# Transposes of the unit matrix between two norms' tiles, a row tile mixed by VectorE alone, and half a unit of keys and values moved behind the branch products

## The chip, the cores and the metric

The kernel runs on one core of one Trainium2 chip. The metric is the device time of one execution in microseconds (us); three runs of the kernel before gave 1453.57, 1454.41 and 1455.25, a median of 1454.41.

## The reference, cut to what matters

Two decoder layers on x of 2 x 256 rows by 512, each of three blocks (self-attention, a block on a context of 2 x 512 rows, a feed-forward block), and each block is followed by `x = layernorm(x + block(x))`. Six such norms are counted here from 0. The change acts in and around these:

```python
# layer 0, third block ("mixing"), then norm 2
H_res, H_pre, H_post = logits of (x * rsqrt(mean(x*x))) @ [W_res, W_pre, W_post].T
H_res = sinkhorn_log(H_res)            # 50 iterations on 4x4 per row
H_res = (1 - g) * I + g * H_res
x_pre = einsum('btnc,btn->btc', x_streams, softmax(H_pre))
y = x_pre @ W_branch
x_mixed = einsum('btij,btjc->btic', H_res, x_streams)     # 4 streams of 128 columns
block = x_mixed + einsum('btc,btn->btnc', y, softmax(H_post))
x = layernorm(x + block)               # norm 2

# layer 1, first block: a gated linear attention; it begins with
dt = softplus(x @ Win.T + dt_bias);  g = dt * A           # 32 heads
x = layernorm(x + l1_attention(x))     # norm 3

# layer 1, second block: cross-attention to the context
q = x @ Wq.T;  k = ctx @ Wk.T;  v = ctx @ Wv.T            # 8 groups of keys and values
```

The keys and values of the cross-attention depend on the context alone, so the kernel computes them early, beside the Sinkhorn iterations.

## The kernel before

The 512 rows are four tiles of 128 rows (`t` = 0 to 3), held in `x`; `xT` holds the columns as rows. The programs of the engines are written out one by one, in the order in which each engine works, and semaphores tie them together; there is no scheduler. The order of each engine's program is thus the order of the calls at the end of the kernel (`block.tensor` for TensorE, and so on).

**Norm n** runs in two pairs of tiles (`PAIRS`). VectorE takes the statistics (`ln_spread`), GpSimd the power (`ln_gpsimd`, L718), VectorE scales the two tiles (`ln_rows`, L712), TensorE transposes each in four pieces (`ln_tensor`, L725), and ScalarE copies the result to `xT` (`ln_scalar`, L765). After norm 3 ScalarE writes a high part and VectorE the low part (L737), and the cross-attention's queries (L192 to L194, three products of parts for each) start when both are there.

**The mixing layer.** TensorE computes the logits from `xT` pair by pair (`mix_logits`, L945) and the branch products of all four tiles (`mix_branches`, L953, one bank of `BRANCH_BANKS` for each tile). VectorE runs 50 Sinkhorn iterations in five windows (`sink_rounds`, L1138, L1142, L1144), GpSimd gathers the factors (L1129), and between two windows ScalarE takes their logarithm (L1195) and a new exponential (L1197), for which VectorE waits. ScalarE scales the branch products (`branch_pre`, L1152), TensorE sums them (`mix_branch_sums`, L1824), and ScalarE writes the result of each stream to `tmp[4 + t]` (`branch_post`, L1159). At the end of the iterations VectorE mixes the four streams of each tile: ScalarE has made the products of streams 0 and 1 (`mix_streams`, L997), VectorE those of streams 2 and 3 with a running sum (L1108) and adds ScalarE's two (L1100). The statistics of norm 2 (L1088) stand between the tiles.

**Keys and values.** There are 32 units (8 groups of 4), each sixteen 128x256 products on TensorE that fill a bank (`kv_unit`, L1803) and two copies on ScalarE (`kv_copy`, L1838). Units 0 and 1 stand ahead of the loop, in banks 0 and 3 (`kv_tensor_first`, `KV_FIRST`), the rest in `kv_tensor` alternates between banks 2 and 7, so a unit waits for the copy of the one two before it. ScalarE's copies are dealt out over the five windows of the Sinkhorn iterations by `KV_WINDOWS`; a window's copies, the branch work and `mix_streams` all stand in its queue ahead of the window's logarithm:

```python
KV_WINDOWS = [3, 5, 5, 6, 11]
for i, count in enumerate(KV_WINDOWS):
    for k in range(count):
        kv_copy(act, unit)
        ...
        if i == 4 and k in (5, 6):
            mix_streams(act, 2 * (k - 5))
            mix_streams(act, 2 * (k - 5) + 1)
```

**After norm 2** TensorE computes the product for dt (`dt_tensor`, L1272, 32x512 in four steps of the contraction), then the values, keys and queries of the first attention group; VectorE and ScalarE make dt's running sums, which go through memory (`g_rows`) and come back as rows for the decays.

Of the kernel before, what the change touches and what calls it, by code (L numbers as in the profile page):

```python
# [14 lines left out]
P = 128  # L15
# [20 lines left out]
def decoder_kernel(nc, a, out):  # L36

    sems = {}
    with ExitStack() as ctx:
# [248 lines left out]

        FILLERS = 10

        def l0_tensor(pe):
# [645 lines left out]

        BRANCH_BANKS = [1, 3, 4, 5]

# [17 lines left out]
        def mix_scalar(act):  # L957
            for k in range(2):
                for t in PAIRS[k]:
                    act.wait_ge(sem("ln_x"), NT * 1 + t + 1)  # L960
                    act.activation(tmp[t][:, :], x[:, t, :], ACT.Square, accum_out=ssq[:, 0, t:t + 1])\
                       .then_inc(sem("mix_ssq"), 1)
                ln_scalar(act, 1, k)
                if k == 0:
                    kv_copy(act, 1)

# [23 lines left out]
        def mix_streams(act, t):  # L990

            if t == 0:
                act.wait_ge(sem("mix_ready"), 3)
                act.wait_ge(sem("branch"), NT + 1)
# [6 lines left out]
        def mix_vector(dve):  # L1001
# [89 lines left out]
            for t in range(NT):  # L1091
                acc = tmp[4 + t]
                at = [0] * STREAMS
                for j in (2, 3):
                    xj = x[:, t, j * P:(j + 1) * P]
                    if j == STREAMS - 1:
                        dve.wait_ge(sem("vector_step"), tally[0])
                        dve.wait_ge(sem("branch_part"), 2 * NT + t + 1)
                        for part in mixed:
                            step(dve, dve.tensor_tensor(acc[:, :], acc[:, :], part[t], ALU.add))  # L1100
                        at = [tally[0]] * STREAMS
                    for i in range(STREAMS):
# [53 lines left out]
        def branch_post(act, t):  # L1156

            for i in range(STREAMS):
                last = act.activation(tmp[4 + t][:, i * P:(i + 1) * P], bank[6][:, t * P:(t + 1) * P],  # L1159
                                      ACT.Copy, scale=soft[:, 0, t * 8 + 4 + i:t * 8 + 5 + i])  # L1160
            last.then_inc(sem("branch_part"), 1)

        def sink_scalar(act):
# [10 lines left out]
            act.activation(h, h, ACT.Exp).then_inc(sem("sink_h"), 1)  # L1174
            unit = len(KV_FIRST)
            for i, count in enumerate(KV_WINDOWS):
                for k in range(count):
# [8 lines left out]
                    if i == 3 and k < 2:  # L1186
                        branch_post(act, k + 2)
                    if i == 4 and k in (5, 6):
                        mix_streams(act, 2 * (k - 5))
                        mix_streams(act, 2 * (k - 5) + 1)  # L1190
                if i < SINK_ITERS // SINK_BLOCK - 1:
# [561 lines left out]
        KV_BANKS = [2, 7]  # L1753
        KV_WINDOWS = [3, 5, 5, 6, 11]
        KV_FIRST = [0, 3]
# [63 lines left out]
        def mix_branch_sums(pe):  # L1819

            for t in range(NT):
                pe.wait_ge(sem("branch_part"), t + 1)
                for j in range(STREAMS):
                    last = pe.matmul(bank[6][:, t * P:(t + 1) * P], ident[:, :], tmp[t][:, j * P:(j + 1) * P],  # L1824
                                     start=(j == 0), stop=(j == STREAMS - 1))
# [757 lines left out]
        def _(pe):  # L2583
# [11 lines left out]
            ln_tensor(pe, 1, 0)  # L2595
            kv_tensor_first(pe, 1, (0, 1))
            mix_logits(pe, 0)
            ln_tensor(pe, 1, 1)
            mix_logits(pe, 1)
            mix_branches(pe)  # L2600
            kv_tensor(pe)
            ln_tensor(pe, 2, 0)
            pe.wait_ge(sem("kv_copied"), 4 * NG)
            ln_tensor(pe, 2, 1)
            dt_tensor(pe)
            l1_tensor(pe)
            for k in range(2):
                ln_tensor(pe, 3, k)
            pe.wait_ge(sem("low_part"), L1_LOW + KC + NG + NT)
# [107 lines left out]
```

## Time and profile before

| | us |
|---|---|
| three runs | 1453.57, 1454.41, 1455.25 |
| profiled execution | 1456.52 |
| its span, first to last instruction | 1454.0 |
| TensorE busy | 1404.8 (97%) |
| VectorE busy | 1065.0 (73%) |
| ScalarE busy | 872.7 (60%) |
| GpSimd busy | 590.3 (41%) |
| share of the chain that ended last | TensorE 70%, VectorE 14%, ScalarE 5%, GpSimd 4% |

The profile is one execution of the program. Times are us from the span's start. PE is TensorE's matmul side, PEld its weight loads, DVE VectorE, ACT ScalarE, POOL GpSimd, SP SyncE. "Granted clock" is the share of full speed that TensorE was allowed; 1.00 is 2.4 GHz and 0.50 is 1.2 GHz. Ends of matmuls are modelled, so starts are the better marks. Where a row has "[a <-b]", the engine was idle for a us before it, until b.

### The profile page before, as it was taken

The numbers are of one execution on the slowest core, as the hardware profiler recorded it, in microseconds if no ns is written. First come the engines' busy times: TensorE is split into PE (matmuls) and PEld (weight loads), VectorE is DVE, ScalarE is ACT, GpSimd is POOL, SyncE is SP. The second block draws the span as 40 slices with busy tenths as digits, with TensorE's granted clock in tenths as the row PEclk, the third lists the DMA queues.
The fourth block names the chain that finished last, engine by engine and source line by source line (L and its number), as shares of the span: only waits on it lengthen the run. The fifth ranks groups of instructions, "written<-read, shape, count | busy, mean of one in ns | idle before, by whom it ended". The sixth has DMA issues, their size and how long they took to land.

```text
span 1454.0 us, 24444 instructions
## 1 busy us (share of the span) xinstructions
PE 1404.8 (97%) x7666; PEld 1175.8 (81%) x7666; DVE 1065.0 (73%) x2471; ACT 872.7 (60%) x2194; POOL 590.3 (41%) x631
## 2 busy tenths in 40 slices
PE   8999999999999899999999999889999999999997
PEld 7888888887788767778788788678888888888875
DVE  5697667687787876766776776767788788777885
ACT  5556555655423456755755755647677677677661
POOL 3555444444122136555645645425243242242221
PEclk9999999999999989999999999989999999999999
DMA  8011110112123230321322221320111012012000
GB/s 325 1 73 73 73 71 2 71 34 102 59 89 128 99 135 30 130 102 42 119 101 76 82 102 59 131 77 25 36 67 74 16 73 87 15 72 79 1 1 30
DMA packets 30135, 107.75 MB, mean 74 GB/s; under 512 B 3847, under 2 KB 13191, under 8 KB 22104
## 3 DMA queue, kind: packets, MB, share of 16 engines
q1 hardware_dynamic: 30040, 106.58, 20.0%
q8 instruction: 47, 0.77, 0.2%
q14 instruction: 48, 0.39, 0.1%
HBM read 97.07 MB, written 9.50 MB: 73 GB/s over the span
## 4 chain that ended last, share of the span: by engine, by line
PE 70%; DVE 14%; issue 6%; ACT 5%; POOL 4%; DMA 0%; DVEq 0%; POOLq 0%; ACTq 0%; SPq 0%
PE bank L192 14%; PE bank L193 14%; PE bank L194 14%; PE bank L1803 5%; PE bank L1974 3%; POOL wq_low L1244 2%; PE bank L336 2%; PE bank L1989 2%; PE bank L1995 2%; PE bank L359 2%; PE bank L1991 2%; PE bank L305 2%; PE bank L1932 1%; DVE logit L2286 1%; PE bank L347 1%
## 5 line engine op out<-in xcount | busy, mean ns | idle before, releaser
L165 POOL TENSOR_TENSOR tmp<-tmp,sin 128x512 f32<-128x512 f32 x80 | 106.5, 1332 | 220.0 <-ACT tmp L150 218.1
L194 PE MATMUL bank<-wo_low,att_high 128*128 128x512 f32 x384 | 150.7, 392 | 0.0
L2286 DVE SCALAR_TENSOR_TENSOR logit<-bank,qss,amask 128x512 f32<-128x512 f32 x128 | 91.0, 747 | 58.7 <-PE bank L194 57.6
L2192 POOL TENSOR_TENSOR qss<-qss,half 128x4 f32<-128x4 f32 x32 | 34.9, 1091 | 201.2 <-DVE qss L2272 201.2
L1803 PE MATMUL bank<-kT,wg 128*128 128x256 f32 x512 | 113.7, 384 | 2.9 <-ACT prob L1838 2.9
L2093 ACT ACTIVATE prob<-logit,rmax 128x512 f32<-128x512 f32 x128 | 91.6, 719 | 38.7 <-DVE rmax L2290 38.7
L1803 PEld LDWEIGHTS bank<-kT,wg 128*128 128x128 f32 x512 | 97.9, 192 | 17.4 <-ACT prob L1838 3.7
L149 ACT ACTIVATE tmp<-bank 64x512 f32<-64x512 f32 x80 | 47.6, 595 | 103.8 <-PE bank L194 98.1
L192 PE MATMUL bank<-l_wo_high,att_high 128*128 128x512 f32 x256 | 104.6, 408 | 1.8 <-DVE att_low L1687 1.1
L193 PE MATMUL bank<-xT_high,wq_low 128*128 128x512 f32 x256 | 103.4, 404 | 0.0
L193 PE MATMUL bank<-l_wo_high,att_low 128*128 128x512 f32 x256 | 99.8, 390 | 0.0
L2107 ACT ACTIVATE p_high<-bank 128x512 fp32r<-128x512 f32 x128 | 70.1, 597 | 45.6 <-PE bank L1974 45.2
L580 DVE TENSOR_TENSOR logit<-bank,keys 128x384 f32<-128x384 f32 x64 | 35.5, 555 | 73.2 <-PE bank L338 73.2
L194 PEld LDWEIGHTS bank<-wo_low,att_high 128*128 128x128 f32 x384 | 72.1, 188 | 16.6
L2304 DVE TENSOR_TENSOR p_low<-bank,p_high 128x512 fp32r<-128x512 f32 x128 | 81.8, 681 | 0.1
L2290 DVE TENSOR_REDUCE rmax<-logit 128x2 f32<-128x1024 f32 x64 | 78.1, 1220 | 2.2
L448 ACT ACTIVATE prob<-logit,rmax 128x128 f32<-128x128 f32 (+1 forms) x128 | 57.4, 449 | 33.4 <-DVE rmax L584 33.3
L228 DVE TENSOR_TENSOR x<-x,bank 128x512 f32<-128x512 f32 x96 | 64.7, 680 | 17.2 <-PE bank L194 16.6
L2099 ACT ACTIVATE prob<-prob,rsum 128x512 f32<-128x512 f32 x64 | 46.4, 724 | 39.7 <-DVE rsum L2295 39.7
L1989 PE MATMUL bank<-p_high,v_high 128*128 128x256 f32 x256 | 67.9, 297 | 2.1 <-ACT p_high L2107 2.1
L1974 PEld LDWEIGHTS bank<-ident,prob 128*128 128x128 f32 x512 | 59.4, 140 | 11.9 <-issue 2.3
L1974 PE MATMUL bank<-ident,prob 128*128 128x128 f32 x512 | 67.5, 273 | 1.5 <-DVE k_low L2260 1.4
(321 smaller groups left out, 4393.5 us busy)
## 6 DMA issues: line engine op xcount, KB each, us to landing
wq<-in_l_wq SPq DMA_DIRECT2D x16, 1024.0 KB, 5.8
wo<-in_l_wo SPq DMA_DIRECT2D x16, 1024.0 KB, 4.9
wkv<-in_l_wkv SPq DMA_DIRECT2D x16, 512.0 KB, 5.7
wg<-in_l_wg SPq DMA_DIRECT2D x8, 1024.0 KB, 4.8
wq<-in_x_wq SPq DMA_DIRECT2D x8, 1024.0 KB, 7.1
wo<-in_x_wo SPq DMA_DIRECT2D x8, 1024.0 KB, 4.9
kT<-in_x_wkv SPq DMA_DIRECT2D x8, 512.0 KB, 3.9
kv_keys<-logit SPq DMA_DIRECT2D x8, 512.0 KB, 4.4
```

The costliest lines, as they stand in the source:

```text
L165: eng.tensor_tensor(halves(tmp[4 + j % 2]), halves(tmp[2 + j % 2]), per_batch(sin), ALU.mult).then_inc(sem(f"{l}_sinp"), 1)
L192: eng.matmul(dst, a_high, b_high, start=start, stop=False)
L193: eng.matmul(dst, a_low, b_high, start=False, stop=False)
L194: return eng.matmul(dst, a_high, b_low, start=False, stop=stop)
L1803: last = pe.matmul(dst[:, i * 256:(i + 1) * 256], wg[t // CT][:, c, t % CT * P:(t % CT + 1) * P], weights[:, c, :], start=(c == 0), stop=( ...
L1974: last = pe.transpose(bank[5 + half_][:, kt * L + c * P:kt * L + (c + 1) * P], prob[s % 2][:, c, (2 * half_ + kt) * P:(2 * half_ + kt + 1) ...
L1989: pe.matmul(dst, v_high[at][:, b * CT + kt, :], p_high[s % 2][:, kt, :], start=(kt == 0), stop=False)
L2093: last = act.activation(prob[s % 2][:, c, :], logit[s % 2][:, c, :], ACT.Exp, bias=rmax[s % 2][:, c:c + 1], accum_out=rsum[s % 2][:, c:c + 1])
L2107: act.activation(p_high[s % 2][:, 2 * half_:2 * half_ + 2, :].rearrange("p a b -> p (a b)"), bank[5 + half_][:, :], ACT.Copy).then_inc(sem ...
L2286: dve.scalar_tensor_tensor(logit[s % 2][:, c, :], bank[3 + c][:, :], qss[p][:, 1, h, 2 * b + c:2 * b + c + 1], amask[:, c, :], ALU.mult, A ...
L2290: dve.tensor_reduce(rmax[s % 2][:, 0:2], logit[s % 2][:, :, :], AX.X, ALU.max, negate=True)\
L2304: dve.tensor_tensor(p_low[s % 2][at].rearrange("p a b -> p (a b)"), bank[5 + half_][:, :], p_high[s % 2][at].rearrange("p a b -> p (a b)") ...
```

## The change

- A helper `keep_busy` issues transposes of the unit matrix into a bank that nobody reads. In norm 2, 14 of them stand behind the first pair of tiles and 6 behind the second. In norm 3, 16 stand behind the first pair, after a wait for the last residual sum of tile 2 (whose bank they write), and 11 behind the second pair.
- The second half of unit 1 moves behind the branch products; its copy moves from ScalarE's norm 1 into the first window. The branch banks change to 1, 4, 5 and 6, since bank 3 is still in use, and the branch sums go to bank 1.
- The windows of copies become 5, 5, 5, 6 and 10.
- VectorE makes all four streams of tile 0; ScalarE makes streams 0 and 1 of tiles 1, 2 and 3 only, one tile behind each of three copies, the first of them one copy earlier in the window.

```diff
+        def keep_busy(pe, n, dst):
+            for _ in range(n):
+                pe.transpose(dst[:, 0:P], ident[:, :], ident[:, :])
...
-        BRANCH_BANKS = [1, 3, 4, 5]
+        BRANCH_BANKS = [1, 4, 5, 6]
+        BRANCH_SUMS = 1
...
                 ln_scalar(act, 1, k)
-                if k == 0:
-                    kv_copy(act, 1)
...
         def mix_streams(act, t):
-            if t == 0:
+            if t == 1:
                 act.wait_ge(sem("mix_ready"), 3)
...
-                for j in (2, 3):
+                for j in (range(STREAMS) if t == 0 else (2, 3)):
                     xj = x[:, t, j * P:(j + 1) * P]
                     if j == STREAMS - 1:
                         dve.wait_ge(sem("vector_step"), tally[0])
-                        dve.wait_ge(sem("branch_part"), 2 * NT + t + 1)
-                        for part in mixed:
-                            step(dve, dve.tensor_tensor(acc[:, :], acc[:, :], part[t], ALU.add))
-                        at = [tally[0]] * STREAMS
+                        if t:
+                            dve.wait_ge(sem("branch_part"), 2 * NT + t)
+                            for part in mixed:
+                                step(dve, dve.tensor_tensor(acc[:, :], acc[:, :], part[t], ALU.add))
+                            at = [tally[0]] * STREAMS
...
-            unit = len(KV_FIRST)
+            unit = 1
...
-                    if i == 4 and k in (5, 6):
-                        mix_streams(act, 2 * (k - 5))
-                        mix_streams(act, 2 * (k - 5) + 1)
+                    if i == 4 and k in (4, 5, 6):
+                        mix_streams(act, k - 3)
...
-        KV_WINDOWS = [3, 5, 5, 6, 11]
+        KV_WINDOWS = [5, 5, 5, 6, 10]
...
             ln_tensor(pe, 1, 0)
-            kv_tensor_first(pe, 1, (0, 1))
+            kv_tensor_first(pe, 1, (0,))
             mix_logits(pe, 0)
             ln_tensor(pe, 1, 1)
             mix_logits(pe, 1)
             mix_branches(pe)
+            kv_tensor_first(pe, 1, (1,))
             kv_tensor(pe)
             ln_tensor(pe, 2, 0)
+            keep_busy(pe, 14, bank[1])
             pe.wait_ge(sem("kv_copied"), 4 * NG)
             ln_tensor(pe, 2, 1)
+            keep_busy(pe, 6, bank[1])
             dt_tensor(pe)
             l1_tensor(pe)
-            for k in range(2):
-                ln_tensor(pe, 3, k)
+            ln_tensor(pe, 3, 0)
+            pe.wait_ge(sem("l1_added"), 4 * (NG - 1) + 3)
+            keep_busy(pe, 16, bank[L1_OUT[2]])
+            ln_tensor(pe, 3, 1)
+            keep_busy(pe, 11, bank[L1_OUT[2]])
```

**TensorE from norm 1 to the units of keys and values**, before (L725 is a tile's transposes, L1803 products of a unit, L945 the logits, L953 a tile's branch products):

```order
L725 MATMUL bank6<-ident,x 128x128 x4
L725 MATMUL bank5<-ident,x 128x128 x4
L1803 MATMUL bank3<-kT0,wg0 128x256 x8
L945 MATMUL bank0<-wmix,xT 128x24 x8
L725 MATMUL bank7<-ident,x 128x128 x4
L725 MATMUL bank2<-ident,x 128x128 x4
L945 MATMUL bank0<-wmix,xT 128x24 x8
L953 MATMUL bank1<-branch,xT 128x128 x4
L953 MATMUL bank3<-branch,xT 128x128 x4
L953 MATMUL bank4<-branch,xT 128x128 x4
L953 MATMUL bank5<-branch,xT 128x128 x4
L1803 MATMUL bank2<-kT0,wg1 128x256 x8
```

The same place in the change, where the lines are L730, L1807, L951 and L959:

```order
L730 MATMUL bank6<-ident,x 128x128 x4
L730 MATMUL bank5<-ident,x 128x128 x4
L1807 MATMUL bank3<-kT0,wg0 128x256 x4
L951 MATMUL bank0<-wmix,xT 128x24 x8
L730 MATMUL bank7<-ident,x 128x128 x4
L730 MATMUL bank2<-ident,x 128x128 x4
L951 MATMUL bank0<-wmix,xT 128x24 x8
L959 MATMUL bank1<-branch,xT 128x128 x4
L959 MATMUL bank4<-branch,xT 128x128 x4
L959 MATMUL bank5<-branch,xT 128x128 x4
L959 MATMUL bank6<-branch,xT 128x128 x4
L1807 MATMUL bank3<-kT0,wg0 128x256 x4
```

Four of the eight products of unit 1 in bank 3 have moved from ahead of the first logits to behind the last branch products. (A row counts the products of the program; the profile has two records for such a product.)

**VectorE at the start of the mix**, before (L1108 multiplies and adds, L1100 adds ScalarE's products):

```order
L1108 SCALAR_TENSOR_TENSOR tmp4<-x,hres,tmp4 128x128 x4
L1100 TENSOR_TENSOR tmp4<-tmp4,tmp0 128x512
L1100 TENSOR_TENSOR tmp4<-tmp4,xT 128x512
L1108 SCALAR_TENSOR_TENSOR x<-x,hres,tmp4 128x128 x4
L1108 SCALAR_TENSOR_TENSOR tmp5<-x,hres,tmp5 128x128 x4
```

and in the change (L1113 and L1105):

```order
L1113 SCALAR_TENSOR_TENSOR tmp4<-x,hres,tmp4 128x128 x12
L1113 SCALAR_TENSOR_TENSOR x<-x,hres,tmp4 128x128 x4
L1113 SCALAR_TENSOR_TENSOR tmp5<-x,hres,tmp5 128x128 x4
L1105 TENSOR_TENSOR tmp5<-tmp5,tmp1 128x512
L1105 TENSOR_TENSOR tmp5<-tmp5,xT 128x512
```

Tile 0 has lost its two additions of ScalarE's products and gained eight products of its own; tile 1 is as before.

**TensorE at norm 2**, in the change (L730 are the tiles' transposes, L294 those of the unit matrix, L1276 the product for dt):

```order
L730 MATMUL bank6<-ident,x 128x128 x4
L730 MATMUL bank5<-ident,x 128x128 x4
L294 MATMUL bank1<-ident 128x128 x14
L730 MATMUL bank7<-ident,x 128x128 x4
L730 MATMUL bank2<-ident,x 128x128 x4
L294 MATMUL bank1<-ident 128x128 x6
L1276 MATMUL bank7<-xT,win 32x512 x4
```

The rows of L294 are new; before, the four rows of transposes and the product for dt followed each other directly.

## Rows read from the trace of the kernel before

**Rows 1.** The page, 40 slices of the span: granted clock in tenths.

```profile
PEclk9999999999999989999999999989999999999999
```

**Rows 2.** Timeline, all engines: start, us, engine, line, operation, shapes, idle before.

```profile
380.50 3.62 PE L1803 MATMUL bank<-kT,wg 128*128 128x256 f32 x16
...
383.31 1.00 DVE L712 TENSOR_SCALAR x<-x,mv,lnr 128x512 f32<-128x512 f32 x2 [0.81 <-POOL lnr L718]
383.96 1.86 PE L945 MATMUL bank<-wmix,xT 128*128 128x24 f32 x16
...
384.70 0.63 ACT L961 ACTIVATE tmp<-x 128x512 f32<-128x512 f32 x1
...
386.33 1.08 ACT L765 ACTIVATE xT<-bank 128x512 f32<-128x512 f32 x2 [0.30 <-PE bank L725]
```

**Rows 3.** Timeline: TensorE's unit 7, and ScalarE's second and fourth logarithm.

```profile
411.94 5.41 PE L1803 MATMUL bank<-kT,wg 128*128 128x256 f32 x16 [2.07 <-ACT prob L1838]
...
429.11 0.23 ACT L1195 ACTIVATE zsm<-fac 128x32 f32<-128x32 f32 x1 [0.58 <-POOL fac L1129]
...
466.79 0.23 ACT L1195 ACTIVATE zsm<-fac 128x32 f32<-128x32 f32 x1 [0.28 <-POOL fac L1129]
```

**Rows 4.** Timeline: the mix, 486 to 505 us.

```profile
486.33 1.14 DVE L1108 SCALAR_TENSOR_TENSOR tmp<-x,hres,tmp 128x128 f32<-128x128 f32 x4
...
487.12 1.27 ACT L997 ACTIVATE tmp<-x,hres 128x128 f32<-128x128 f32 x4
...
489.65 0.69 DVE L1100 TENSOR_TENSOR tmp<-tmp 128x512 f32<-128x512 f32 x1 [2.19 <-ACT xT L997]
...
492.24 1.13 DVE L1108 SCALAR_TENSOR_TENSOR tmp<-x,hres,tmp 128x128 f32<-128x128 f32 x4
...
497.69 7.17 PE L1803 MATMUL bank<-kT,wg 128*128 128x256 f32 x32 [0.80 <-ACT prob L1838]
```

**Rows 5.** Timeline: norm 2 and the product for dt.

```profile
506.25 1.11 PE L725 MATMUL bank<-ident,x 128*128 128x128 f32 x8 [1.39 <-DVE x L712]
...
506.95 1.08 ACT L765 ACTIVATE xT<-bank 128x512 f32<-128x512 f32 x2 [1.39 <-PE bank L725]
...
509.18 1.94 PE L725 MATMUL bank<-ident,x 128*128 128x128 f32 x8 [1.82 <-DVE x L712]
...
511.90 5.50 PE L1272 MATMUL bank<-xT,win 128*32 128x512 f32 x8 [0.78 <-ACT xT L765]
```

**Rows 6.** Windows: length, busy PE, PEld, DVE, ACT, POOL; granted clock, DMA, GB/s.

```profile
506.20:508.90 2.70, 1.11 (x8) 0.84 (x8) 1.85 (x6) 1.08 (x2) 0.70 (x1) 1.00 0.97 361
509.00:515.60 6.60, 5.64 (x13) 2.45 (x14) 3.13 (x7) 5.04 (x11) 0.00 (x0) 0.50 0.46 171
...
956.20:962.80 6.60, 5.62 (x13) 4.46 (x14) 2.12 (x4) 0.19 (x2) 0.00 (x0) 0.50 0.20 86
...
932.20:935.50 3.30, 2.91 (x14) 2.94 (x14) 1.45 (x6) 0.00 (x0) 2.90 (x3) 0.50 0.96 333
935.70:937.00 1.30, 1.30 (x15) 1.30 (x13) 0.75 (x1) 1.30 (x8) 0.38 (x1) 1.00 0.95 372
1416.90:1420.30 3.40, 2.35 (x16) 1.81 (x15) 1.51 (x4) 2.93 (x7) 2.41 (x2) 1.00 0.00 0
```

**Rows 7.** Timeline: transposes of TensorE in two of these stretches.

```profile
934.43 1.06 PE L1451 MATMUL bank<-ident,q 128*128 128x128 f32 x4
...
1417.35 1.09 PE L1974 MATMUL bank<-ident,prob 128*128 128x128 f32 x8
```

**Rows 8.** Timeline: norm 3's second pair and the first query product.

```profile
954.51 1.11 PE L725 MATMUL bank<-ident,x 128*128 128x128 f32 x8 [2.58 <-DVE x L712]
...
957.18 0.80 PE L192 MATMUL bank<-xT_high,wq_high 128*128 128x512 f32 x1 [1.56 <-DVE xT_low L737]
```

**Rows 9.** The chain that ended last, the queries: start, us, line.

```profile
958.40 0.43 PE bank L194
...
963.06 0.23 PE bank L193
```

More of the change, by code:

```diff
@@ L1158, in branch_post @@
             for i in range(STREAMS):
-                last = act.activation(tmp[4 + t][:, i * P:(i + 1) * P], bank[6][:, t * P:(t + 1) * P],
+                last = act.activation(tmp[4 + t][:, i * P:(i + 1) * P], bank[BRANCH_SUMS][:, t * P:(t + 1) * P],
                                       ACT.Copy, scale=soft[:, 0, t * 8 + 4 + i:t * 8 + 5 + i])
@@ L1823, in mix_branch_sums @@
                 for j in range(STREAMS):
-                    last = pe.matmul(bank[6][:, t * P:(t + 1) * P], ident[:, :], tmp[t][:, j * P:(j + 1) * P],
+                    last = pe.matmul(bank[BRANCH_SUMS][:, t * P:(t + 1) * P], ident[:, :], tmp[t][:, j * P:(j + 1) * P],
                                      start=(j == 0), stop=(j == STREAMS - 1))
```

## The prediction

> **What bounds the kernel now.** I read the page first: the granted clock of TensorE is below 9 tenths in two slices of 40 only, the fifteenth and the twenty-seventh [rows 1], so on the whole TensorE is fed and runs at its upper level, 2.4 GHz. Those two slices hold norms 2 and 3. I then read the timeline where the change acts: the front of the mixing layer (380 to 389 us), the units of keys and values beside the Sinkhorn rounds (to 505 us), and the two norms. Up to 486 us two chains run side by side. VectorE does 50 Sinkhorn rounds and stops four times for a logarithm of ScalarE; TensorE does units of keys and values, each copied out by ScalarE. What ends last is VectorE: TensorE waits for its rows before the transposes of norm 2 [rows 5]. From there on TensorE, ScalarE and VectorE hand the work to each other, and the clock has fallen to 1.2 GHz: the stretch from 509.0 to 515.6 us is granted 0.50, behind one with 1.11 us of work in 2.70. So it is after norm 3, from 956.2 to 962.8 us [rows 6].
>
> **Part 1, half a unit of keys and values behind the branch products.** Before, unit 1 takes TensorE from 380.50 to 383.96, 3.46 us, and the transposes of tiles 2 and 3 stand behind it; ScalarE also copies it before it squares tile 2 at 384.70 [rows 2]. Now half of it (1.73) stands there: TensorE is free at 382.2, the first logits end at 383.9, and the transposes follow. VectorE's norm has tile 2 ready at 383.85 (383.31 and half of the 1.00 for two), so ScalarE squares from there. For both squares it needs some 1.3 us (384.70 to 386.33 less 0.30 idle), which puts the first column copy at 385.15 instead of 386.33. The logits end 1.2 us earlier, and so the Sinkhorn chain starts.
> How much of that reaches the end of the rounds depends on ScalarE's queue: a window's last copy stands ahead of the logarithm that VectorE waits for. TensorE starts the branch products 1.2 us earlier and does half a unit more behind them. With five copies in the first window instead of three it no longer waits 2.07 us before unit 7, nor does it run that unit in 5.41 us instead of 3.46 [rows 3], as that slow stretch follows the wait. So unit n+1 is done within 0.1 us of where unit n was. The windows also end one unit later (10, 15 and 21 instead of 9, 14 and 20): their last copies end at the old times, 428.5 and 466.5 (the logarithms of 429.11 and 466.79 less idle times of 0.58 and 0.28 [rows 3]). Of 1.2 us only 0.6 is then left at the second logarithm and 0.3 at the fourth. **The rounds end 0.3 us earlier** (bounds 0 and 0.6).
>
> **Part 2, tile 0 by VectorE alone.** Before, VectorE does one stream of tile 0 at 486.33 and then waits 2.19 us for ScalarE's products; two sums and the last stream bring it to tile 1 at 492.24, 5.91 us later [rows 4]. ScalarE copies a unit first and starts its products at 487.12. Now VectorE does sixteen products, 1.14 per four: 4.3 to 4.6 us. It saves 5.91 - 4.3 = 1.6 us. In that time ScalarE does tile 1 (eight products, two rows of 1.27), and it copies one unit between any two tiles, where pairs of tiles had made TensorE wait 0.80 us at 497.69 [rows 4]. Tiles 1 to 3 find their products ready. **The rows of norm 2 come 1.6 + 0.3 = 1.9 us earlier**: its transposes start at 504.35 instead of 506.25, and could at 507.3 instead of 509.18 [rows 5].
>
> **Part 3, norm 2.** TensorE's last unit now ends near 500.4 (504.86 less one unit of 3.46, less the wait of 0.80, plus bits), so it waits 4 us for VectorE instead of 1.39. I expect it to be at 1.2 GHz when the rows come, or to fall at once: 1.39 and 1.82 us of waiting [rows 5] were enough before. Eight transposes take 1.11 us at 2.4 GHz and 1.94 at 1.2 [rows 5], so 0.14 and 0.24 each. Behind the first eight stand 14 more. At full clock they take 1.9 us and just fit between the pairs of tiles; at half clock they take 3.4. In time: transposes to 506.3, ten fillers at 0.24 to 508.7, where I let the clock rise (an estimate: 0.50 lasted 3.3 us where work filled it, 6.6 where waits were in it [rows 6]), and four at 0.14: 509.25. That is where the second pair starts now: **the fillers eat the lead of 1.9 us**. But the second pair then runs at full clock: 1.78 us from its start to the end of ScalarE's second copy (506.25 to 506.95 + 1.08 for the first pair) and 0.13 to the next product, so 511.15 against 511.90. The six fillers (0.8) fit under those copies. The product for dt took 5.50 us from 511.90, of it 3.7 at 0.50 [rows 5, 6]; at full clock that is 3.5. It ends at 514.65 instead of 517.4. **Norm 2 gives 2.8 us.** Bounds: 4.7 if the clock never falls, 2.0 if it stays low through all the fillers and rises behind them. What follows (dt on VectorE, rows through memory, decays) starts from that product, and its other inputs move with it.
> Can such transposes hold or raise the clock? From 932.2 to 935.5 TensorE is granted 0.50 and ends that stretch with 1.06 us of transposes; behind it the clock is 1.00. From 1416.9 to 1420.3 it has 2.35 us of work, 1.09 of it transposes, and stays at 1.00 [rows 6, 7]. I take it that they count. The Trainium skill says otherwise: by "TensorE: Matmul & The Clock Gate", Part 4 (PE-mode transpose), the full clock does not come from transposes, which don't count as busy in the way of matmuls. By that rule this part would lose; rival 2 has the price, from rows.
>
> **Part 4, norm 3.** TensorE waits 2.58 us between the pairs of tiles and 1.56 before the queries [rows 8]. Sixteen fillers (2.2) fit into the first wait, eleven (1.5) into the second. The new wait, for the sum of tile 2, costs nothing: that sum feeds this norm and is done before tile 3's. The clock should hold. The queries start at 957.18 and step by 0.43 us, from 963.06 by 0.23 [rows 8, 9]: some thirteen steps that take 5.9 us and would take 3.3 with the slower first one. **It gives 2.5 us**; bounds 1.3 (the low stretch can fall shorter than here) and 2.9.
>
> **Sum.** 2.8 + 2.5 = 5.3 us off the profiled execution of 1456.5 (a span of 1454.0 and 2.5 around it): 1451.2. The median of the runs, 1454.4, lies 2.1 below that execution. The low stretches fall a little differently from run to run, so I take 5.0 off the median: **1449.4 us**. This case's own range is 1447.4 to 1451.4.
>
> **Rivals.**
> 1. *The fillers hold the clock but do not raise it* (12%). Norm 3 gives its 2.5. In norm 2 the clock is down after the wait of 4 us; fillers run to 509.7, the second pair to 511.6, six fillers to 513.1, the product takes 5 to 6 us: 518.1 to 519.1, a loss of 1.2. Together 1.3 faster: 1453.1. For it: no row shows transposes alone raising the clock. Against it: the row at 932.2.
> 2. *The fillers count for nothing and stand in the way at half speed* (10%), the slower side. Norm 2 loses up to 1.7 (519.1). In norm 3 the clock falls near 956 as before; eleven fillers take 2.6 instead of 1.5 and push the queries back by 1.1. Together 2.8 slower: 1457.2, and up to 1459 if the sixteen are caught too. It decides where 14 fillers at 0.24 outlast the gap of 1.8 us between the pairs.
> 3. *The clock stays up in norm 2 in spite of the wait* (8%): 4.7 + 2.5, so 1447.2.
> 4. *The gains are there, but behind norm 2 the gate weights or the rows through memory bind* (6%): norm 3's 2.5 alone, 1451.9.
>
> **How the numbers follow.** The forecast has 64%. A measurement of this kernel can tell about 0.2%, 2.9 us, from no change. Faster by more, below 1451.5: nearly all of the forecast, rival 3, a third of rival 4 and a tenth of rival 1: 0.73. Within it: most of rivals 1 and 4, half of 2: 0.21. Slower: half of rival 2 and one more in a hundred: 0.06. The range, 1447.0 to 1453.5, takes in the forecast and rivals 1, 3 and 4, and leaves out rival 2 and the tails.
>
> **What would show it.** In the changed profile: the Sinkhorn rounds start 1.2 us earlier, but the fourth logarithm only 0.3, right behind a copy; no stop of TensorE near 410 us; VectorE without a wait in the mix; TensorE idle for about 4 us before norm 2 and granted 0.50 there, its 14 fillers partly at 0.24; the dt product in 3.5 us; 1.00 throughout norm 3 and query steps of 0.23. Wrong would be: 0.50 to the end of the dt product (rivals 1, 2), query steps of 0.43 (rival 2), a wait of VectorE for ScalarE's products, or the logarithms later than before.

## The result, and the profile after

The changed kernel takes 1461.58 us (median of 20 runs), the kernel before 1454.53 (20 runs): a ratio of 1.0042 with a 95% interval of 1.0034 to 1.0049. It is slower; 1449.4 was forecast, with 1453.5 as the upper end. The profiled execution has a span of 1459.3 us against 1454.0. Where the 5.3 us arise, read from the timelines of the two executions (us from the start of each span):

| point in the program | before | after | difference |
|---|---|---|---|
| VectorE reads the logits (the rounds start) | 389.05 | 389.28 | +0.23 |
| last instruction of the rounds | 486.01 | 488.68 | +2.67 |
| first transposes of norm 2 | 506.25 | 507.37 | +1.12 |
| first product behind the dt product | 517.34 | 516.88 | -0.46 |
| first product of the last attention group | 879.11 | 885.89 | +6.78 |
| last group's second set of transposes (before L1451) | 937.22 | 945.47 | +8.25 |
| first query product | 957.18 | 965.45 | +8.27 |
| end of the span | 1454.0 | 1459.3 | +5.3 |

Step by step, the change gives 1.55 us in the mix, 1.58 in norm 2 and 2.97 from the first query product on (2.60 of it in the queries right behind norm 3, the rest because later low stretches of the clock fell elsewhere). It loses 0.23 ahead of the rounds, 2.44 in them, 7.24 among the attention groups, which it does not touch, and 1.47 in the last of these.

**The logits of norm 1.** Timeline of the changed kernel, TensorE and VectorE, and one window (length; busy PE, PEld, DVE, ACT, POOL; granted clock):

```profile
383.17 1.00 DVE L717 TENSOR_SCALAR x<-x,mv,lnr 128x512 f32<-128x512 f32 x2 [0.81 <-POOL lnr L723]
385.62 3.56 PE L951 MATMUL bank<-wmix,xT 128*128 128x24 f32 x16 [0.74 <-ACT xT L770]
389.00 5.50 PE L959 MATMUL bank<-branch,xT 128*128 128x128 f32 x32
389.28 0.69 DVE L1018 SCALAR_TENSOR_TENSOR mix<-bank,ssq,base 128x24 f32<-128x24 f32 x4 [3.99 <-PE bank L951]
...
385.80:392.40 6.60, 6.60 (x32) 6.60 (x33) 2.31 (x13) 1.04 (x5) 0.57 (x1) 0.50 0.00 0
```

The second logits product starts 1.36 us earlier than before (386.98, [rows 2]), but behind a wait of 0.74 us instead of 0.25, and the clock is 0.50 from 385.7 us for 6.8 us. The product takes 3.56 us instead of 1.97 and the branch products 5.50 instead of 3.82 (before: "388.79 3.82" in the same view), so the lead is gone, and units of keys and values start 1.89 us later (394.33 against 392.44).

**The logarithms.** ScalarE, second and fourth window:

```profile
431.20 0.38 ACT L1842 ACTIVATE prob<-bank 128x256 f32<-128x256 f32 x1
431.46 0.23 ACT L1199 ACTIVATE zsm<-fac 128x32 f32<-128x32 f32 x1
...
469.45 0.23 ACT L1199 ACTIVATE zsm<-fac 128x32 f32<-128x32 f32 x1
```

Both stand in ScalarE's queue with no idle time ahead of them (the row above the first is a unit's copy): it is the copies that VectorE waits for. They come 2.35 and 2.66 us later than those of [rows 3].

**The mix and norm 2.** VectorE, then TensorE, then two windows:

```profile
489.00 3.24 DVE L1113 SCALAR_TENSOR_TENSOR tmp<-x,hres,tmp 128x128 f32<-128x128 f32 x12
492.27 1.14 DVE L1113 SCALAR_TENSOR_TENSOR x<-x,hres,tmp 128x128 f32<-128x128 f32 x4
493.33 1.14 DVE L1113 SCALAR_TENSOR_TENSOR tmp<-x,hres,tmp 128x128 f32<-128x128 f32 x4
...
507.37 1.11 PE L730 MATMUL bank<-ident,x 128*128 128x128 f32 x8 [3.97 <-DVE x L717]
508.31 2.92 PE L294 MATMUL bank<-ident 128*128 128x128 f32 x14
511.03 1.51 PE L730 MATMUL bank<-ident,x 128*128 128x128 f32 x8
512.38 0.82 PE L294 MATMUL bank<-ident 128*128 128x128 f32 x6
513.36 3.59 PE L1276 MATMUL bank<-xT,win 128*32 128x512 f32 x8 [0.16 <-ACT xT L770]
...
508.70:511.90 3.20, 3.20 (x17) 3.20 (x17) 1.09 (x3) 0.44 (x1) 0.69 (x1) 0.50 0.61 241
512.20:517.00 4.80, 4.64 (x19) 1.68 (x17) 2.65 (x6) 4.80 (x11) 0.00 (x0) 1.00 0.00 0
```

VectorE no longer waits in the mix: tile 0 takes 4.33 us (489.00 to 493.33) instead of 5.91 [rows 4]. TensorE waits 3.97 us instead of 1.39 [rows 5], starts the transposes at full clock, falls to 0.50 at 508.6, and is at 1.00 again from 512.0. The dt product takes 3.59 us instead of 5.50.

**The loop over the attention groups.** Between two groups of layer 1, VectorE's timeline after, and its DMA queues from 736 to 753 us:

```profile
740.34 0.69 DVE L228 TENSOR_TENSOR x<-x,bank 128x512 f32<-128x512 f32 x1 [2.03 <-PE bank L194]
744.87 0.87 DVE L1699 COPY gc<-cols 128x40 f32 x1 [3.84 <-issue]
750.74 1.14 DVE L1646 SCALAR_TENSOR_TENSOR probT<-logit,gc,lower 128x128 f32<-128x128 f32 x4 [5.00 <-issue]
...
q14 instruction: 4, 0.03, 0.5%
```

and before, the same place (in its DMA view of that stretch there is no row of q14):

```profile
740.86 0.69 DVE L228 TENSOR_TENSOR x<-x,bank 128x512 f32<-128x512 f32 x1 [2.03 <-PE bank L194]
741.47 0.18 DVE L1695 COPY gc<-cols 128x40 f32 x1
741.89 1.14 DVE L1642 SCALAR_TENSOR_TENSOR probT<-logit,gc,lower 128x128 f32<-128x128 f32 x4 [0.24 <-DVE gc L1695]
```

"issue" is an idle time in which the engine waited for nothing that the profile shows. VectorE runs the middle four groups as a loop of two passes over two groups each (`piped_groups`, L138), 266 instructions a pass, and its only jump back lies here, in a stop of 3.84 us; one of 5.00 follows. Meanwhile four packets of 8 KB arrive on q14, a queue of instructions (the profile does not say of which engine), one of them within each stop. TensorE runs dry behind it and comes back at half clock:

```profile
756.22 0.79 PE L192 MATMUL bank<-l_wg_high,xT_high 128*128 128x512 f32 x1 [4.76 <-ACT tmp L152]
...
754.40:761.00 6.60, 4.78 (x11) 3.80 (x12) 5.88 (x10) 5.01 (x9) 3.46 (x3) 0.50 0.22 93
```

The group in which this happens takes 60.10 us, where all others but the first (44.8) take 52.8 to 52.9. Over the whole span the page counts 53 packets on q14 after and 48 before.

**Norm 3.** TensorE, after:

```profile
959.16 1.03 PE L730 MATMUL bank<-ident,x 128*128 128x128 f32 x8
960.03 1.91 PE L294 MATMUL bank<-ident 128*128 128x128 f32 x16
962.78 1.11 PE L730 MATMUL bank<-ident,x 128*128 128x128 f32 x8 [0.84 <-DVE x L717]
963.73 1.36 PE L294 MATMUL bank<-ident 128*128 128x128 f32 x11
965.45 0.50 PE L192 MATMUL bank<-xT_high,wq_high 128*128 128x512 f32 x1 [0.36 <-DVE xT_low L742]
965.79 0.40 PE L193 MATMUL bank<-xT_high,wq_low 128*128 128x512 f32 x1
...
955.00:972.00 17.00, 15.80 (x95) 13.36 (x94) 10.49 (x24) 4.57 (x13) 3.51 (x5) 1.00 0.34 125
```

The waits of 2.58 and 1.56 [rows 8] have become 0.84 and 0.36 and the clock is 1.00 throughout. The queries step by 0.23 from the second on, where thirteen of them stepped by 0.43 before [rows 9].

### The profile page after: what moved, and what is told of

Read it like the earlier page. It is cut to its first block, busy times and chain, and to the rows that moved or that the text cites. A ratio compares the mean times of both kernels' runs of the same rounds, so it can differ in the third digit from the quotient of the medians.

```text
span 1459.3 us, 24535 instructions
## 1 busy us (share of the span) xinstructions
PE 1409.5 (97%) x7713; PEld 1183.2 (81%) x7713; DVE 1065.7 (73%) x2477; ACT 870.3 (60%) x2186; POOL 590.0 (40%) x631
## 4 chain that ended last, share of the span: by engine, by line
PE 68%; DVE 15%; issue 6%; ACT 6%; POOL 4%; DMA 0%; DVEq 0%; ACTq 0%; POOLq 0%; SPq 0%
PE bank L192 13%; PE bank L193 13%; PE bank L194 13%; PE bank L1807 5%; PE bank L1978 3%; POOL wq_low L1248 2%; PE bank L341 2%; PE bank L1993 2%; PE bank L1999 2%; PE bank L364 2%; PE bank L1995 2%; PE bank L310 2%; DVE logit L2290 1%; PE bank L1936 1%; PE bank L352 1%
## 5 line engine op out<-in xcount | busy, mean ns | idle before, releaser
L1807 PE MATMUL bank<-kT,wg 128*128 128x256 f32 x512 | 111.4, 379 | 0.0
L1807 PEld LDWEIGHTS bank<-kT,wg 128*128 128x128 f32 x512 | 97.0, 190 | 13.3 <-issue 0.2
## 6 DMA issues: line engine op xcount, KB each, us to landing
wkv<-in_l_wkv SPq DMA_DIRECT2D x16, 512.0 KB, 5.9
kT<-in_x_wkv SPq DMA_DIRECT2D x8, 512.0 KB, 4.2
kv_keys<-logit SPq DMA_DIRECT2D x8, 512.0 KB, 4.7
```

Source lines behind the costliest of these rows:

```text
L1807: last = pe.matmul(dst[:, i * 256:(i + 1) * 256], wg[t // CT][:, c, t % CT * P:(t % CT + 1) * P], weights[:, c, :], start=(c == 0), stop=( ...
```

## The experiments

**Theory A: the place of VectorE's loop.** The change puts a few more instructions on VectorE ahead of the loop. Its body would then start at another place against the blocks in which instructions are fetched, and at a bad one the jump back would find part of the body gone. The rival: the stops come from the products, transposes or DMAs of the change. Both are separated by memsets of a column of a spare tile, which stand ahead of `dt_vector` and compute nothing.

*e1: the change with twelve such memsets; e2: the kernel before with five (the same lines with `range(5)`).*

```python
+            for i in range(12):
+                dve.memset(spare[:, i:i + 1], 0.0)
             dve.wait_ge(sem("ld_l1"), 16 * 4)
             dt_vector(dve)
```

> The changed kernel with twelve one-column memsets on VectorE between norm 2 and the product for dt, where VectorE waits. Theory A (VectorE's loop over the attention groups now lies so in its code that the jump back finds its first instructions gone and loads them again: two stops of 4 to 5 us at 740 and 746 us, with extra instruction packets at 737 to 752): the loop moves by 12 instructions, the stops go, group 4 takes 52.8 us instead of 60.1, and the kernel is 7 us faster than the change, about 1454 us, ratio to before 0.997 to 1.000. Rival B (the stops come from a late input or from DMA traffic at that time, not from where the code lies): they stay, ratio 1.004.

> The kernel before with five such memsets, about the number of instructions that the change adds ahead of VectorE's loop. Theory A: the same two stops appear in group 4 though nothing else of the change is there, 7 us slower, ratio about 1.005. Rival B: no stops, ratio 1.000.

e1: 1451.81 us (12 runs), 0.9988 of before (0.9976 to 0.9999), all groups behind the first 52.8 to 52.9. e2: 1460.49 us (5 runs), 1.0042 (1.0029 to 1.0055), with both stops. VectorE's timeline at the jump, e1 and then e2:

```profile
739.13 0.69 DVE L229 TENSOR_TENSOR x<-x,bank 128x512 f32<-128x512 f32 x1 [2.03 <-PE bank L195]
739.78 0.18 DVE L1700 COPY gc<-cols 128x40 f32 x1
740.21 1.14 DVE L1647 SCALAR_TENSOR_TENSOR probT<-logit,gc,lower 128x128 f32<-128x128 f32 x4 [0.24 <-DVE gc L1700]
```

```profile
737.63 0.69 DVE L229 TENSOR_TENSOR x<-x,bank 128x512 f32<-128x512 f32 x1 [2.03 <-PE bank L195]
742.10 0.93 DVE L1696 COPY gc<-cols 128x40 f32 x1 [3.78 <-issue]
747.80 1.14 DVE L1643 SCALAR_TENSOR_TENSOR probT<-logit,gc,lower 128x128 f32<-128x128 f32 x4 [4.77 <-issue]
```

Adding instructions takes the loss away, and five that do nothing bring it into the kernel before. The rival falls. (By medians e1 is 9.8 us faster than the change, and the group explains 7.3 of it. In e1's profile the clock also stayed up until the logits of norm 1 were through; the rest is not assigned.)

*e8 and e9: the kernel before with nine and with fourteen memsets.*

> The kernel before with nine memsets. If VectorE's code is loaded in blocks and what counts is how many blocks its loop body of 266 instructions touches, the bad positions are a run of about nine beginning at one to five more than before, so nine more is bad too: group 4 takes 60.1 us, span about 1460. If the position of five was a single bad one, it takes 52.8, span about 1454.

> Fourteen one-column memsets on VectorE ahead of its loop over groups, in the kernel before. If the place of the loop's body against blocks of fetched instructions decides (4.8 to 5 and 9 added instructions had the stops, 0 and, in another version, some 17 had not), 14 should lie past the bad stretch: all groups 52.8 us, no stop of VectorE of 3.8 and 4.8 us behind the branch, about 1454 us. If more instructions alone are bad, or if the count matters in another way, one group takes 60.1 us and the run 1460.

One run each: e8 1459.8 us, one group of 60.22, and the two stops are one of 9.85 us with two packets of q14 in it; e9 1454.67, all groups behind the first 52.8 to 52.9, no stop. So 0 is good, 5 and 9 are bad, 14 is good: what counts is the place, not that there are more instructions. What is shown is this, and that packets of an instruction queue arrive within the stops. That VectorE waits for them is the plain reading, but no run shows it directly. The Trainium skill, "Runtime: NRT & Kernel Launch", section "Instruction fetch mechanics", says that a taken branch to code outside a window of two pages must wait for a fetch; the stops agree with it. It gives blocks of 16 KiB with 256 instructions; the packets here carried 8 KB, which by its ratio is 128 instructions. Two estimates follow. In pages of 256, a body of 266 instructions lies in two pages or, from nine starts in 256, in three; in blocks of 128 it lies in three or, from nine starts in 128, in four. The four points fit a bad stretch of nine and do not tell the two apart; how many blocks VectorE holds was not measured.

**The parts, apart from it.** e3 and e4 leave the loop at its place of before; e5, e6, e7, e10, e11 and e12 have the twelve memsets. None of these eight shows the stops.

*e3: the fillers of norms 2 and 3 alone, in the kernel before.*

```python
             ln_tensor(pe, 2, 0)
+            keep_busy(pe, 14, bank[1])
...
             ln_tensor(pe, 2, 1)
+            keep_busy(pe, 6, bank[1])
...
+            keep_busy(pe, 16, bank[L1_OUT[2]])
...
+            keep_busy(pe, 11, bank[L1_OUT[2]])
```

> The kernel before with only the transposes of the unit matrix, 14 and 6 in norm 2, 16 and 11 in norm 3. Theory A (they hold the clock where the wait ahead of them is 1.4 us and not 4): granted clock 1.00 through both norms, second pair of norm 2 at 509.2, dt product in 3.5 us, queries in steps of 0.23: 2.8 + 2.5 us faster, ratio 0.9963. Rival C (transposes do not count as work for the clock): 0.50 as before in both, 0 to 3 us slower.

1451.07 us (10 runs), 0.9977 (0.9967 to 0.9986). TensorE in norm 2, and the window from there to the next group:

```profile
506.22 1.11 PE L730 MATMUL bank<-ident,x 128*128 128x128 f32 x8 [1.40 <-DVE x L717]
507.17 1.69 PE L294 MATMUL bank<-ident 128*128 128x128 f32 x14
509.15 1.06 PE L730 MATMUL bank<-ident,x 128*128 128x128 f32 x8 [0.29 <-DVE x L717]
510.05 0.82 PE L294 MATMUL bank<-ident 128*128 128x128 f32 x6
511.04 3.59 PE L1277 MATMUL bank<-xT,win 128*32 128x512 f32 x8 [0.17 <-ACT xT L770]
...
508.00:515.00 7.00, 6.54 (x33) 3.36 (x32) 3.97 (x8) 5.19 (x11) 0.42 (x1) 1.00 0.58 203
```

With the rows at the time of before (506.22), the clock is at 1.00, and the next product comes at 514.57 instead of 517.34: 2.77 us. Both norms were seen to gain as expected, but the ratio over the runs is 3.3 us (1454.95 x 0.0023), less than expected. The profiled span is 7.4 us shorter than before's: it is the second fastest of the ten runs, and it also lacks the low stretches of the clock that before has near 932 and 987 us.

This one execution does not show by itself that the fillers held the clock. In e2, which has none, the profiled execution has 1.00 throughout norm 2 as well (TensorE, and one window):

```profile
505.70 1.11 PE L726 MATMUL bank<-ident,x 128*128 128x128 f32 x8 [1.41 <-DVE x L713]
508.62 1.06 PE L726 MATMUL bank<-ident,x 128*128 128x128 f32 x8 [1.82 <-DVE x L713]
510.52 3.59 PE L1273 MATMUL bank<-xT,win 128*32 128x512 f32 x8 [0.83 <-ACT xT L766]
...
505.00:515.00 10.00, 6.66 (x32) 3.45 (x33) 6.59 (x21) 6.47 (x13) 0.88 (x2) 1.00 0.59 211
```

It takes all profiles together, seven of either kind, one execution each (all in us):

| norm 2 | wait ahead of the transposes | low stretch of the clock | dt product | first transposes to next product |
|---|---|---|---|---|
| no fillers: before, e2, e4, e8, e9 | 1.4 | 6.8, none, 3.4, 6.8, 6.8 | 5.50, 3.59, 4.90, 5.18, 5.46 | 11.1, 8.3, 9.7, 10.8, 11.0 |
| no fillers: e6, e12 | 2.6, 4.0 | 10.2, 10.2 | 6.46, 6.50 | 12.0, 12.1 |
| fillers: e3, e5, e7 | 1.4, 2.1, 0.8 | none | 3.59 | 8.4, 8.4, 8.3 |
| fillers: e10, e11, the change | 2.6, 2.6, 4.0 | 3.4 | 3.59 | 9.5 |
| fillers: e1 | 4.0 | 6.8, from within the wait | 3.59 | 10.4 |

With fillers the dt product ran at full clock in all seven; without them in one of seven.

*e4: the half unit alone; e7: the change, twelve memsets, and the old ends of the windows.*

e4 is the kernel before with the change's edits of unit 1, the banks and `KV_WINDOWS`, and with `mix_streams` in pairs at k of 4 and 5. e7, in the kernel of e1:

```python
-        KV_WINDOWS = [5, 5, 5, 6, 10]
+        KV_WINDOWS = [4, 5, 5, 6, 11]
-                    if i == 4 and k in (4, 5, 6):
-                        mix_streams(act, k - 3)
+                    if i == 4 and k in (5, 6, 7):
+                        mix_streams(act, k - 4)
```

> The kernel before with only the half unit moved, the branch banks and the windows of copies. Theory A (without the half unit TensorE has too little work between norm 1 and the branch products, its clock falls to 1.2 GHz there, the logits gain nothing, and with one unit more per window each logarithm waits for its copy): Sinkhorn rounds end 2 to 3 us later (488.3 to 489.3 instead of 486.3), 1.5 to 3 us slower, ratio 1.001 to 1.002. Rival D (the clock's fall there was chance in one execution): rounds end 0.3 us earlier, ratio 0.999 to 1.000.

> The changed kernel with the twelve memsets (as e1) and windows of 4, 5, 5, 6 and 11 copies, so that they end at units 4, 9, 14 and 20 as before. Theory A (the later unit at each window's end makes VectorE wait): logarithms are no longer right behind a copy; where the clock holds at 385 us, the rounds end 1.2 us before the kernel before (484.8 to 485.2) against 486.3 in e1; about 1 us faster than e1: 1450.8, ratio 0.998. Rival F (ScalarE's queue does not bind): as e1.

e4: 1455.43 us (11 runs), 1.0006 (0.9995 to 1.0017): the half unit alone brings nothing. e7: 1450.60 us (8 runs), 0.9973 (0.9963 to 0.9984). The second logarithm in e7, with ScalarE idle ahead of it:

```profile
428.88 0.38 ACT L1843 ACTIVATE prob<-bank 128x256 f32<-128x256 f32 x1
429.76 0.23 ACT L1200 ACTIVATE zsm<-fac 128x32 f32<-128x32 f32 x1 [0.50 <-POOL fac L1135]
```

From the start to the end of the rounds it is 96.96 us before, 96.95 to 96.98 in e5, e6 and e7, but 99.40 in the change, 99.35 in e1 and 99.56 in e4, which have windows of [5, 5, 5, 6, 10]. One copy fewer ahead of each logarithm gives back 2.4 us, although the clock fell in e7 at 387.6 as well, and TensorE's units start 5.8 us behind the first read of the logits there (5.0 to 5.2 in the change, e1 and e4, 3.4 before). No run has the windows of the change with the clock up through the branch products, so what they cost then is open.

*e5: the change without the half unit (unit 1 and the windows as before), twelve memsets; e6: tile 0 alone.*

e6 is the kernel before with the change's edits of VectorE's mix and of `mix_streams` (at k of 5, 6 and 7), and the memsets. e5 has the branch banks, the bank of the branch sums and the place of unit 1's copy as before, `mix_streams` at k of 5, 6 and 7, and, in the kernel of e1:

```python
-        KV_WINDOWS = [5, 5, 5, 6, 10]
+        KV_WINDOWS = [3, 5, 5, 6, 11]
...
-            kv_tensor_first(pe, 1, (0,))
+            kv_tensor_first(pe, 1, (0, 1))
...
-            kv_tensor_first(pe, 1, (1,))
```

> Fillers in both norms and tile 0 by VectorE alone, unit 1 whole and the windows of copies as before, the products of tiles 1, 2, 3 behind units 26, 27, 28, and twelve memsets so that VectorE's loop does not lie badly. Theory A (the half unit does harm, the rest adds up): rounds end at 486.0 as before, rows of norm 2 1.6 us earlier, clock 1.00 through both norms: 1.6 us better than the fillers alone (1451.1), so 1449.5, ratio 0.9965. Rival E (without the half unit TensorE's last units end so near the rows that the 1.6 us are lost to them, or VectorE's rows are late for another reason): as the fillers alone, 0.9977.

> Only tile 0 by VectorE alone, with the products of tiles 1, 2, 3 behind units 26, 27, 28 and the twelve memsets. Theory A: VectorE waits for nothing in the mix, rows of norm 2 at 504.6 instead of 506.25, 1.6 us faster less what the clock gives or takes in norm 2: ratio 0.9985 to 0.9993. Rival E: nothing, 1.000.

e5: 1450.36 us (11 runs), 0.9966 (0.9957 to 0.9975). e6: 1452.41 us (11 runs), 0.9992 (0.9982 to 1.0003). In e6 the rounds end at 486.37 (0.36 later than before) and the transposes start at 505.04 (1.21 earlier): tile 0 is worth 1.57. But little is left of it at the next product (517.08 against 517.34), because in this execution the clock is low for 10.2 us instead of 6.8:

```profile
505.04 1.11 PE L726 MATMUL bank<-ident,x 128*128 128x128 f32 x8 [2.56 <-DVE x L713]
507.97 1.94 PE L726 MATMUL bank<-ident,x 128*128 128x128 f32 x8 [1.81 <-DVE x L713]
510.69 6.46 PE L1273 MATMUL bank<-xT,win 128*32 128x512 f32 x8 [0.78 <-ACT xT L766]
...
506.40:516.00 9.60, 7.25 (x15) 2.79 (x16) 3.86 (x20) 5.92 (x12) 1.71 (x2) 0.50 0.34 122
```

*e12: e1 without the fillers of norm 2.*

```python
-            keep_busy(pe, 14, bank[1])
-            keep_busy(pe, 6, bank[1])
```

> The kernel of e1 (the change, with 12 memsets for the place of the loop) without the 14 and 6 transposes of norm 2; the 16 and 11 of norm 3 stay. If those of norm 2 raise the clock and so shorten the product for dt: the clock is 0.50 through the dt product, next product at 517.0 (as in e6) instead of 515.4, some 1.6 us slower than e1's profile (1451.8 to 1453.5). If they only stand in the way: 1450 to 1451.5, and the next product no later than 515.4. Norm 3 at 1.00 and query steps of 0.23 in both.

1455.34 us (10 runs), 0.9991 (0.9978 to 1.0003). Its runs lie in two clusters, four from 1450.6 to 1452.1 and six from 1455.3 to 1456.1; those of e1 do too (six from 1450.1 to 1450.9, five from 1455.1 to 1456.4, one at 1452.7). So the two kernels' times are not told apart by these runs. The profile is of the upper cluster, and its norm 1 is like that of the change (0.50 from 385.8, transposes at 507.40): the clock is 0.50 from 508.7 for 10.2 us, and the next product starts at 519.47, 2.59 later than in the change. Of that, 0.55 is given back before the next group starts (44.20 us against 44.75). The first mechanism expected holds; the time was 1.8 above its upper end.

*e10: the kernel of e7 again; e11: with five fillers in norm 1.*

```python
             ln_tensor(pe, 1, 1)
+            keep_busy(pe, 5, bank[4])
             mix_logits(pe, 1)
```

> Placeholder: the kernel of e7 again, one look. Theory: the fall of the clock in norm 1 differs from run to run of the same kernel, so 1448 to 1452 us; if the fall is at 387.6 again the logits come at 389.7, if not at 387.0 to 387.5.

> The kernel of e7 with five transposes of the unit matrix behind the transposes of tiles 2 and 3 of norm 1, in the 0.73 us in which TensorE waits for ScalarE's column copy. If a falling clock there costs the half unit its gain and the transposes hold it: second logits product behind the wait in 1.9 instead of 2.8 us, VectorE's rounds start at 387.3 instead of 389.7, end 97.0 later (484.3), transposes of norm 2 start at 503.0, product for dt ends near 511.5 instead of 513.7; 1449 us against 1450.6 of e7 (up to 2 us less). If the 24-column products of the logits, not the wait, let the clock fall: 0.50 from 387 or so as in e7, and 1450.6.

e10: 1447.23 us, one run, below the range that I had given. e11: 1449.26 us (5 runs), 0.9958 (0.9944 to 0.9973). In e11:

```profile
382.43 1.00 DVE L718 TENSOR_SCALAR x<-x,mv,lnr 128x512 f32<-128x512 f32 x2 [0.81 <-POOL lnr L724]
384.88 1.97 PE L952 MATMUL bank<-wmix,xT 128*128 128x24 f32 x16 [0.19 <-ACT xT L771]
386.95 0.69 DVE L1019 SCALAR_TENSOR_TENSOR mix<-bank,ssq,base 128x24 f32<-128x24 f32 x4 [2.40 <-PE bank L952]
```

From VectorE's scaled rows to the logits it is 4.52 us instead of 5.74 before and 6.11 in the change: that is the half unit's gain of 1.22, when the clock holds. But e10 shows 4.53 and a clock of 1.00 there without fillers (382.74 to 387.27). So whether the five hold the clock, or the clock did not fall in that run by its own timing, stays open. e11 has the lowest ratio of all and beats both kernels; its interval overlaps those of e5 and e7, so it isn't shown to be faster than those.

**The clock in norm 1, over all profiles.** From VectorE's scaled rows of tiles 2 and 3 to its first read of the logits, with half a unit ahead: 6.11 us (the change), 6.08 (e12), 5.94 (e4), 5.39 (e7), 4.52 (e1 and e11), 4.53 (e10). With the whole unit: 5.73 to 5.75 (before, e2, e3, e6), 5.84 (e9), 6.12 (e8), 6.22 (e5). So the clock falls there in some executions of either kind: before the logits are read in four of seven with half a unit, in three of seven with the whole one (386.4 in e8, 387.4 in e5, 388.2 in e9). That is too few to say that the half unit makes it fall.

## Why the prediction was wrong

**The step that failed most** stands behind Part 3: "What follows (dt on VectorE, rows through memory, decays) starts from that product, and its other inputs move with it." I carried the gain through eight groups unchanged. One of them takes 7.3 us more, for a cause outside every edit, a number of instructions ahead of a loop. No rival named it. I had counted what the moved instructions cost and not where they leave the code behind them. e1 and e2 show it from both sides. Without it the change would stand at about 1454.3 (1461.6 less 7.3), level with the kernel before.

The two profiled executions give the whole error: the change ends 5.3 us later where 5.3 earlier was forecast. Of these 10.6 us, 7.2 are the loop, 2.3 arise up to the first product behind the dt product (0.5 earlier instead of 2.8), 1.5 are a longer low stretch of the clock in the last group, and norm 3 with what follows gave 0.5 more than forecast.

**Part 1** was wrong too: "The rounds end 0.3 us earlier (bounds 0 and 0.6)"; they end 2.67 later. The arithmetic of instructions held: 1.22 us between scaled rows and logits where the clock stays up (e10, e11). What I missed is the clock in norm 1. The shorter TensorE queue leaves a wait of 0.74 us ahead of the second logits product, and the clock fell right behind it in the change, e4 and e12 (385.7, 386.1, 385.8 us), and at 387.5 and 387.6 in e1 and e7. That the wait is the cause is not shown: e10 has the wait and no fall, e5 and e8 have a wait of 0.25 and the fall. In the change the fall took the lead of 1.2 us, and TensorE's units start 1.89 us later instead of earlier. The sentence "their last copies end at the old times, 428.5" had no slack for it: the copy ended at 431.58. By the counts of the change, TensorE had gained 4.0 us from the stop near 410 that went away, as forecast, and lost 1.73 to the half unit and 1.89 to the later start; 0.4 was left, and one more unit ahead of the logarithm needs 3.46. With windows that end one unit earlier (e7) this costs nothing. So the term was 3.0 us off: 1.4 in the start of the rounds (0.23 later instead of 1.2 earlier) and 1.5 in VectorE's waits for copies (2.4 instead of 0.9). I had read the clock at norms 2 and 3 and not at norm 1, and a forecast by one execution could not have known it: the kernel of e7, run again as e10, has no fall there.

**Part 2** was right: 1.6 forecast, 1.55 measured in the change and 1.57 in e6, VectorE without a wait. Its 1.9 in all became a loss of 1.12 with Part 1.

**Part 3** was right in mechanism, and its duration a little long. The clock fell behind the first transposes, fourteen fillers ran in part at half speed, it rose behind them, and the dt product took 3.59 (forecast 3.5). From the first transposes to the next product I had 10.3 us, measured 9.51 in the change, 9.53 in e11, 10.43 in e1, 8.35 in e3 and e5, 8.34 in e7, and 11.09 before. "The fillers eat the lead of 1.9 us" holds only in part: where the clock fell ahead of or in them they cost some 1.2 us (9.5 against 8.35) or 2.1 (e1). In e5, behind a wait of 2.1 us, it stayed up as in rival 3, and all of a lead of 1.96 us over e3 arrived (transposes at 504.26 against 506.22, next product at 512.61 against 514.57). Without fillers, behind the same norm 1, the clock stays at 0.50 for 10.2 us (e12) instead of 3.4. With this and the table under e3, rivals 1 and 2 are refuted: in no profile with fillers was the clock low in the dt product. What the fillers of norm 2 are worth in the time of runs is not shown, as e1 and e12 are not told apart. The Trainium skill's rule that I had cited against this part ("TensorE: Matmul & The Clock Gate", Part 4 (PE-mode transpose)) is not borne out by these rows.

**Part 4** was right: 2.5 forecast (bounds 1.3 and 2.9), 2.60 measured over the first twenty queries in the change. The 2.97 from there to the end hold 0.4 more, for which the fillers need not be the cause.

**The sum** nearly comes, once the two faults are mended: 1450.6 in e7, 1450.4 in e5 (without Part 1) and 1449.3 in e11 (with five more fillers), against a forecast of 1449.4. It is not the forecast's sum part by part, as e7 has no lead from Part 1 (rounds start at 389.70) and loses nothing of Part 2 to fillers; that these come out alike is in part luck. That gains were real and that the changed kernel is slower are both true.

What stays unexplained is the spread of 5 us within e1 and e12. One part is seen: in the last group the clock falls between 926 and 939 us in every profile but e3's, for 3.4 us in before, e2, e6, e7, e9, e10 and e12, and for 6.8 us in the change, e1, e4, e5, e8 and e11. Counted from the start of that group, its second set of transposes comes at 57.7 us in e3, at 58.1 to 58.7 with the short stretch and at 59.3 to 59.6 with the long one. Norm 1 adds up to 1.6 (6.11 less 4.52). Whether these two make the clusters was not tried.

## What to carry to other kernels

An edit moves all the code behind it. Where an engine's loop has a body of some hundred instructions, read its jump back after every edit: a stop ended by "issue" with packets of an instruction queue in it points to a fetch, and a few dummy instructions ahead of the loop tell it from causes that do not hang on the code's place. Where a queue is shortened so that a wait opens in it, read the clock there in several executions: here a fall took the 1.2 us that the shortening gave in some and not in others. A gain ahead of a wait can be lost to a longer low stretch behind it (e6, one execution). And one profile does not show that an edit holds the clock: e2 had 1.00 through norm 2 with no fillers.

## What the runs showed of the hardware

- Transposes go with a high clock and let it rise: with those of the unit matrix in norm 2 the dt product took 3.59 us in seven profiles of seven, without them in one of seven (4.90 to 6.50 in the others), and in the change the clock is 1.00 from 512.0 us behind 3.4 us filled with transposes alone.
- VectorE's jump back in a loop of 266 instructions costs 3.8 and then 4.8 to 5.0 us at a bad place (the change, and 5 more instructions ahead of it), 9.85 in one stop with 9 more, and nothing at a good one (0 and 14). Of the 8.8 us in the change, 7.3 reach the end, as TensorE had queued work for part of it. VectorE's jumps back in layer 0's attention (192.06 us in the change) and in the last loop (1201.20) have no idle time ended by "issue" behind them in the same execution.
- At 1.2 GHz stretches of 3.4, 6.8 and 10.2 us were seen, the same kernel at other times in other runs; in norm 1 a fall cost up to 1.6 us, and in the last group the long stretch cost 0.6 to 1.5 us more than the short one, which makes differences under 0.2% hard to assign to an edit.
